# Sorting tokens to their two experts in a graph-attention and mixture-of-experts kernel on Trainium2

## The reference

```python
x = x + gnn(layernorm(x), inlayer2, adj, ...)
#   h = inlayer2 @ W.T + b;  logits = (h @ w1 + b1)[:, None] + (h @ w2 + b2)[None, :]
#   softmax(leaky_relu(logits) + (-1e9 where adj == 0)) @ layernorm(x)
x = x + ffn(layernorm(x), gate_w, gate_b, W1, b1, W2, b2)
#   probs = softmax(xf @ gate_w + gate_b);  top2_vals, top2_idx = top_k(probs, 2)
#   cw: top2_vals at top2_idx, 0 elsewhere
#   for each expert: out += cw[:, e] * (gelu(xf @ W1[e] + b1[e]) @ W2[e] + b2[e])
```

## Time and profile before

| | |
|---|---|
| three runs | 508.79, 512.33, 513.11 us; median 512.33 |
| profiled execution, span from first to last instruction | 509.6 us; the page gives no other time for it |
| median less that span | 2.7 us |
| TensorE busy / VectorE / ScalarE / POOL | 471.5 / 425.4 / 234.3 / 46.7 us |
| mean granted TensorE clock | 0.980 of 2.4 GHz |
| attention's last result copied by ScalarE | from 320.04 us |

### The profile page before, as it was taken

The page is one execution under the profiler, slowest core; times in us unless marked ns, Lnnn a source line. Parts: engine busy times, 40 slices in busy tenths (PEclk is TensorE's granted clock), DMA queues, the critical chain, the costliest instruction groups (busy, mean ns, idle before and its releaser), DMA issues.

```text
span 509.6 us, 5787 instructions
## 1 busy us (share of the span) xinstructions
PE 471.5 (93%) x1712; PEld 221.2 (43%) x1712; DVE 425.4 (83%) x726; ACT 234.3 (46%) x362; POOL 46.7 (9%) x98
## 2 busy tenths in 40 slices
PE   2799999799979999899998999798999999999996
PEld 2773434245335444454444534343434444444442
DVE  0447679798998998989989897579899898988985
ACT  1539810113200200102001124689888888988883
POOL 8903202001010020020000000100000000000000
PEclk9859999999989999999999999999999999999999
DMA  6999999999809639389000000423443346445520
GB/s 193 183 106 105 105 106 202 168 163 90 76 2 97 66 30 105 31 77 88 0 0 0 1 0 21 153 84 82 104 82 113 124 118 122 84 103 112 126 50 22
DMA packets 35042, 44.49 MB, mean 87 GB/s; under 512 B 2592, under 2 KB 24528, under 8 KB 34768
## 3 DMA queue, kind: packets, MB, share of 16 engines
q0 software_dynamic: 17920, 18.88, 37.4%
q1 hardware_dynamic: 16288, 25.37, 19.7%
q10 hardware_dynamic: 816, 0.03, 0.1%
HBM read 92.38 MB, written 2.23 MB: 186 GB/s over the span
## 4 chain that ended last, share of the span: by engine, by line
PE 55%; DVE 23%; issue 7%; DMA 7%; ACT 6%; DVEq 1%; SPq 0%; ACTq 0%
PE bank L1044 20%; DVE c L828 11%; PE bank L1089 4%; PE bank L1091 4%; PE bank L1090 4%; DMA x<-in_x 4%; PE bank L1078 4%; PE bank L1080 4%; PE bank L1079 4%; DMA share<-in_L_gnn_inlayer 2%; DVE maskT L640 2%; PE bank L966 2%; ACT mask L567 2%; DVE xs L714 2%; DVE maskT L891 2%
## 5 line engine op out<-in xcount | busy, mean ns | idle before, releaser
L1044 PE MATMUL bank<-c,Y 128*128 128x512 f32 x512 | 232.9, 603 | 8.9 <-DVE c L828 8.3
L828 DVE SCALAR_TENSOR_TENSOR c<-g_row,r_col,maskT 128x512 f32<-128x512 f32 (+1 forms) x256 | 182.1, 744 | 17.8 <-PE bank L1044 14.0
L1044 PEld LDWEIGHTS bank<-c,Y 128*128 128x128 f32 x512 | 93.1, 191 | 132.7 <-issue 75.5
L885 DVE TENSOR_TENSOR mask<-mask,share 128x1024 f32<-128x1024 f32 x64 | 78.2, 1223 | 21.0 <-ACT mask L567 18.5
L567 ACT ACTIVATE mask<-bank,b1T 128x512 f32<-128x512 f32 x128 | 83.8, 688 | 22.8 <-PE bank L1080 21.2
L891 DVE TENSOR_TENSOR maskT<-mask,maskT 128x1024 f16<-128x1024 f32 x64 | 78.4, 1225 | 0.0
L574 ACT ACTIVATE maskT<-mask 128x1024 f16<-128x1024 f32 x64 | 67.4, 1053 | 3.2 <-DVE mask L885 3.1
L1089 PE MATMUL bank<-maskT,w2h 128*128 128x512 f16 x128 | 49.1, 383 | 5.7 <-DVE maskT L891 5.2
L1090 PE MATMUL bank<-maskT,w2h 128*128 128x512 f16 x128 | 49.0, 383 | 0.0
L1091 PE MATMUL bank<-maskT,w2l 128*128 128x512 f16 x128 | 49.0, 383 | 0.0
L1078 PE MATMUL bank<-share,w1h 128*128 (+1 forms) x128 | 48.5, 379 | 0.0
(11 more groups left out here) (145 smaller groups left out, 355.4 us busy)
## 6 DMA issues: line engine op xcount, KB each, us to landing
share<-shares SPq DMA_DIRECT2D x16, 1024.0 KB, 8.3
mask<-in_adj POOLq DMA_DIRECT2D x24, 512.0 KB, 17.2
mask<-in_adj POOLq DMA_DIRECT2D x32, 128.0 KB, 25.6
share<-in_L_gnn_inlayer SPq DMA_DIRECT2D x2, 1024.0 KB, 10.0
share<-in_x POOLq DMA_DIRECT2D x8, 256.0 KB, 12.2
out<-c SPq DMA_DIRECT2D x8, 256.0 KB, 3.8
share<-in_L_ffn_W SPq DMA_DIRECT2D x1, 1024.0 KB, 21.6
W_sb<-in_L_gnn_W SPq DMA_DIRECT2D x1, 64.0 KB, 2.0
```

Source lines behind the costliest of these rows:

```text
L828: dve.scalar_tensor_tensor(c[:, k % CR].rearrange("p (s i) -> p s i", i=32), g_row[:, bass.ds(s * ST, ST)].rearrange("p (s i) -> p s i", i ...
L885: dve.tensor_tensor(hw[:, e % 2], h[:, e % 2], wb[:, e].unsqueeze(1).to_broadcast([P, FC, ST]), ALU.mult).then_inc(hw_done, 1)
L1044: mm(bank[:, par, :], Y[:, k], c[:, k % CR], start=(k == 0), stop=(k == NK - 1)).then_inc(c_used, 1)
```

## The change

The experts no longer see every token. Each token's row is written twice to memory, to a place sorted by expert, and the experts work on 46 tiles of 256 sorted rows (27 for the tokens of supertiles 0 to 4, the first group, and 19 for the other three, each expert's part padded to whole tiles).

A row (`rows`, 132 words) holds 128 high and 128 low float16 parts, made as before but not transposed, and the row's own number. After routing, TensorE counts ranks with triangular and all-ones products (`rank`), VectorE turns ranks into row places (`slot_i`) and into the expert of each tile (`expert`). Then:

- POOL writes rows by indirect DMA, 128 at a time, to `sorted_x` (`place_row`, line 501): the first group's 20 chunks once for the first choice and, with 4096 added to their numbers, once for the second. It does so after supertile 6 of the attention has given the places, while supertile 7 runs.
- SP loads a tile (`load_tile`), up to 12 ahead. TensorE transposes it (`turn_x`), ScalarE copies it back (`copy_x`), then `ffn1` with 256 columns, gelu, `high` and `low` (both now on VectorE), and `ffn2` turned about: hidden values stand still and the weights pass, so results come out by token. TensorE and ScalarE read the tile's expert into a register, and weights and biases are addressed by it.
- VectorE adds the split halves of the result out of PSUM (`evict`), and POOL writes 256 result rows, two indirect DMAs, to `choice_y` at the row's number (`place_choice`, line 514). There are 12 buffers.
- Each token's two results are loaded back, weighed by the gate and added to the residual (`load_choices`, `combine`), for five supertiles beside tiles 37 to 41 and for three at the end.
- The second group has 24 row writes (12 chunks, two choices). POOL makes them from tile 18 on, four ahead of each of six tiles' result writes.

All loops are unrolled. The routing of the first group runs in supertile 6 (before: 24 chunks in supertile 7); the low half of six supertiles' rows is made by POOL (`low_rows`).

```diff
-    PEELED = 3
-    LAG = 3
+    LAG = 2
+    RW = D + 4
+    TW = 256
+    TP = TW // P
+    XR = 12
+    YR = 12
+    HR = 3
+    HEAD = 5
+    GROUP = ((0, HEAD * TS), (HEAD * TS, NK))
+    TILES = [(2 * (b - a) * P + E * (TW - 1)) // TW for a, b in GROUP]
+        COMBINE = TILES[0] + 9
+        SECOND = 18
+        STD, LOGIT, EXP, RANK = 2, 7, 9, 15
...
         def _(sp):
-            def share_out(g):
...
-            def share_in(st, half):
...
+            def load_tile(t):
+                if t == 0 or t == TILES[0]:
+                    for s_in in sorted_in[t > 0]:
+                        sp.wait_ge(s_in, 16 * (GROUP[t > 0][1] - GROUP[t > 0][0]))
...
+                if t >= XR:
+                    sp.wait_ge(y_out[(t - XR) % YR], 16 * TP * ((t - XR) // YR + 1))
+                sp.dma_start(xt[:, t % XR].rearrange("p s w -> p (s w)"),
+                             sorted_x[TW * t:TW * t + TW].rearrange("(p s) w -> p (s w)", s=TP)).then_inc(xt_in[t % XR], 16)
...
+            for t in range(NT):
+                load_tile(t)
+                if COMBINE <= t < COMBINE + HEAD:
+                    load_choices(t - COMBINE, TILES[0])
...
         def _(pool):
+            def place_row(r, v, n):
+                pool.indirect_dma_start(out=sorted_x, out_offset=bass.IndirectOffsetOnAxis(ap=slot_i[:, v, n:n + 1].bitcast(U32), axis=0),
+                                        in_=rows_2[:, n - GROUP[1][0]] if (r, v) == (1, 1) else rows[:, n],
+                                        in_offset=None).then_inc(sorted_in[r][v], 16)
...
+            def place_choice(t):
+                pool.wait_ge(y_done, t + 1)
+                for i in range(TP):
+                    pool.indirect_dma_start(out=choice_y, out_offset=bass.IndirectOffsetOnAxis(ap=xt_id[:, t % XR, i, D:D + 1].bitcast(U32), axis=0),
+                                            in_=y_sb[:, t % YR, i], in_offset=None).then_inc(y_out[t % YR], 16)
...
+            pool.wait_ge(slot_ready, 1)
+            for n in range(*GROUP[0]):
+                place_row(0, 0, n)
+            second_ids()
+            for n in range(*GROUP[0]):
+                place_row(0, 1, n)
             pool.wait_ge(xs_ready, NS)
             pool.tensor_copy(x2[:, (NS - 1) * TS:NS * TS, :], xs[:]).then_inc(x2_kept, 1)
+            pool.wait_ge(xld_ready, 2)
+            pool.wait_ge(c_used, NS * NK)
+            pool.tensor_copy(rows_2, rows[:, GROUP[1][0]:NK]).then_inc(ids_moved, 1)
...
+            for t in range(NT):
+                if t == SECOND:
+                    pool.wait_ge(slot_ready, 2)
+                if SECOND <= t < SECOND + 6:
+                    for n in range(GROUP[1][0] + 2 * (t - SECOND), GROUP[1][0] + 2 * (t - SECOND) + 2):
+                        place_row(1, 0, n)
+                        place_row(1, 1, n)
+                place_choice(t)
...
         def _(act):
+            for t in range(NT):
...
+                experts.append(act.value_load(expert[0:1, t:t + 1], min_val=0, max_val=E - 1))
...
+                if t + 1 < NT:
+                    copy_x(t + 1)
+                gelu(t)
...
         def _(dve):
+            def high(t):
+                dve.wait_ge(gelu_done, t + 1)
+                need(dve, ffn2_done, t + 1 - HR)
+                dve.tensor_scalar(hh[:, t % HR], h[:, t % 2], C_SCALE, None, ALU.mult).then_inc(hh_done, 1)
...
+            def evict(t):
...
+                need(dve, y_out[t % YR], 16 * TP * (t // YR))
+                dve.tensor_reduce(y_sb[:, t % YR], both, AX_X, ALU.add).then_inc(y_done, 1)
...
+            for t in range(NT):
+                high(t)
+                if t >= LAG:
+                    evict(t - LAG)
+                low(t)
...
+                if COMBINE + 1 <= t < COMBINE + 1 + HEAD:
+                    combine(t - COMBINE - 1, 0)
+                    combine(t - COMBINE - 1, 1)
+            for t in range(NT - LAG, NT):
+                evict(t)
+            for s in range(HEAD, NS):
+                combine(s, 0)
+                if s > HEAD:
+                    combine(s - 1, 1)
+            combine(NS - 1, 1)
...
         def _(pe):
+                if t == TILES[0]:
+                    pe.wait_ge(expert_ready, 2)
+                experts.append(pe.value_load(expert[0:1, t:t + 1], min_val=0, max_val=E - 1))
+                if t == 0:
+                    turn_x(0)
+                if t + 1 < NT:
+                    turn_x(t + 1)
+                ffn1(t)
+                if t >= LAG:
+                    ffn2(t - LAG)
...
+                if t == RANK:
+                    rank(1)
```

More of the change, by code:

```diff
@@ L600, in _, with copy_x @@
-            for st in range(PEELED):
-                experts(st)
-            with act.Fori(PEELED, NS) as st:
-                experts(st)
-            high(NS * E - 1, E - 1)
-            copy_y(NS - 1)
+            for s in range(1, NS):
+                supertile(s)
+            post_a(NS - 1, 1)
+            act.wait_ge(expert_ready, 1)
+            experts = []
+            def copy_x(t):
+                act.wait_ge(turned_x, t + 1)
+                need(act, h_ready, t - 1)
+                act.activation(xtT[:, t % 2].rearrange("p v t -> p (v t)"), bank[:, 0, 0:TW].bitcast(F16),
+                               ACT.Copy).then_inc(xtT_ready, 1)
@@ L814, in _, with supertile @@
             BN = (12, 13, 17, 18)
             TURNS = (15, 20, 24, 28)
-            def supertile(s, par, n, first=False, last=False):
-                router = route_b(*ROUTE[0])
+            routers = [route_b(r) for r in range(2)]
+            def supertile(s, first=False, last=False):
+                par = s % 2
                 for k in range(NK):
@@ L845, in supertile @@
                         post_b(s - 1, BN.index(k))
-                    if not first and k == 25:
+                    if last and k == 23:
                         post_c(s - 1)
@@ L940, in _ @@
-            for st in range(PEELED):
-                experts(st)
-            with dve.Fori(PEELED, NS) as st:
-                experts(st)
-            low(NS * E - 1, E - 1)
-            add_out(NS - 1)
+            for s in range(NS):
+                supertile(s, first=(s == 0), last=(s == NS - 1))
+            post_0(NS - 1)
+            post_a(NS - 1)
+            post_sum(NS - 1)
+            post_b(NS - 1, 0)
+            dve.wait_ge(post_step, (NS - 1) * POST + 1)
+            post_b(NS - 1, 1)
@@ L1052, in supertile @@
                         post_a(s - 1)
[L1053 removed]
+                    if not first and k == 24:
                         post_b(s - 1)
[L1055 removed]
+                    if not first and k == 27:
                         post_c(s - 1)
[L1057 to L1058 removed]
+                    if s == HEAD + 1 and k == 20:
+                        rank(0)
             pe.wait_ge(b1_copied, 1)
@@ L1133 @@
+            for t in range(NT - LAG, NT):
+                ffn2(t)
 _INS = ["x", "adj", "L0_gnn_inlayer2", "L0_gnn_W", "L0_gnn_b", "L0_gnn_w1", "L0_gnn_b1", "L0_gnn_w2", "L0_gnn_b2",
```

692 lines of the change are left out of this document (363 added, 329 removed).

## The result

The changed kernel takes 567.63 us (median of 4 runs, 566.11 to 568.35) against 511.41 us for the kernel before (median of 4 runs) on the same chip. The ratio is 1.110, with a 95% interval of 1.106 to 1.115. The forecast was 497, its range ended at 540.

What follows compares the result with a forecast made beforehand. TensorE was taken to bound the expert part (189.6 us). Attention ends at 319, first products 329.5, tile 27 at 417.9, tiles and combining 475.4, tail 494.7; with 2.7 more, 497 us (3% faster), range 470 to 540.

Steps and rivals of the forecast that it cites:

- p: Price of one indirect write by POOL, taken as 0.85 us, between 0.54 and 1.3.
- 112 writes on the path: POOL's writes standing in line on the path where p exceeds 0.89: 40 + 36 + 34 + 2.
- step 3: Tiles 0 to 17: 45 us plus 10 woven in, second slots at 384.5; POOL's 36 result writes end at 383.1.
- Rival A: POOL is the bound, p 1.0 or more: time 513 at 1.0, 535 at 1.2; chance 0.26.
- Step 1: Attention, with routing moved earlier and POOL making low halves (under 3 us), ends at 319 (311 to 326).
- VectorE's interference: First 40 row writes, beside two-input VectorE mask steps, would each wait some 0.3 us: 12 us more, 509.
- rival B: The tile itself is dear, c 3 or more, by register loads or lower clock: 516 at 3.0, 535 at 3.5; chance 0.20.
- What is woven in: Beside tiles 0 to 17: ScalarE table loads, the last supertile's normalisation and VectorE routing steps, 10 us.
- c: Time of one tile of 256 sorted tokens, taken as 2.5 us, between 1.65 and 4.35.
- The tail: At the end: two writes and landing 4.2, six loads 9, combine 2.3, store 3.8 us, to 494.7.
- The clock: TensorE's products run near half rate after a wait; each of the two stalls costs 1 to 2 us so.
- Steps 2 and 4: First and second groups' row writes: TensorE stalls 9 us before the first tile and 13 us before tile 27.

Runs made afterwards that it cites:

- the run with five forms: Changed kernel plus twenty extra indirect writes of five row counts and sizes into unread memory, other engines standing still; 592.89 us (one run).
- 16 and 16 version: Changed kernel with groups of 16 and 16 token blocks, bias split and row writes moved, VectorE pausing, second-group copy dropped; 519.70 us, ratio 1.018.

## Why the prediction was wrong

**The term that was mis-sized: p.** "I take 0.85: the middle of the direct ones beside VectorE plus POOL's smallest read of a column." It is 1.27 at rest. The bounds (0.54 to 1.3) held that, though not the 1.37 beside VectorE; the value did not. The nearest rows were direct DMAs, whose pitch said nothing on the fixed work of an indirect one; and "nothing in the rows shows reading 128 offsets to be as dear as that" looked for the price in the offsets, while the run with five forms puts all but some 0.1 us into the instruction itself. With the prediction's own count of 112 writes on the path, 112 x (1.275 - 0.85) = 47.6 us, of which 1.4 fall into the slack that its step 3 had (383.1 against 384.5): 497 becomes 543. Rival A, with a chance of 0.26, said so: place, count and break-even at 1.0. Its reason, VectorE beside POOL, is the smaller part: the price is 1.27 with the other engines at rest.

**The wait that was missing.** Step 1 (attention's end at 319) counted POOL's low halves at under 3 us and did not follow POOL's program to what stands ahead of them: the bias split, with a load behind both weight loads on SP's queue. Its removal gave 17.3 us (14.5 at the first row write) and put the attention's end at 317.4, where the step had 319. Against the forecast's first slots the wait made 13 us.

**The held write.** The prediction left VectorE's interference out of its sum and weighed it in rival A, at 0.3 us for each of 40 writes. The trace shows one write held for 6.7 us more and the others by 0.0 to 0.7. The Trainium skill (SBUF — State Buffer, Who interferes with whom) says that VectorE instructions with two SBUF inputs contend with POOL instructions that read SBUF, and that in VectorE's two-port mode whoever came first blocks the other for one whole instruction. The runs agree in so far as the hold goes with VectorE's run, but it lasted over several of VectorE's instructions, so this rule does not explain it.

**The sum, and what is left.** On the clock of the traced execution 494.7 + 46.2 + 13 + 6.7 makes 560.6 of the 564.4. Most of the rest lies behind tile 27: from there to the last tile's two writes 62.4 us passed, and 57.5 were forecast. The prediction let the tiles set the pace there and counted only the last two of POOL's 44 writes in that stretch. In the trace POOL pauses no longer than 0.31 us from 493.1 to its last write at 548.0: its writes set the pace there too.

**Right, in part by luck.** Step 3: 55 us from the first products to the second slots were forecast, 56 measured (365.6 to 421.6), but the two terms behind it are off in opposite ways. An undisturbed tile takes 1.85 us, not 2.5 (the columns alone were put at 1.65), so rival B (3 or more) is out, and 18 tiles make 33 us, not 45. What is woven in, with the lower clock after the first stall, took the other 23, not 10:

```profile
365.00:391.00 26.00, 19.55 (x152) 14.86 (x153) 13.88 (x35) 17.70 (x33) 4.46 (x5) 0.78 0.23 62
```

The 600 ns register load that the prediction cited from the Trainium skill (DMA: Bandwidth & Descriptors, Latency and other measured facts) would have made c 2.95; no run here shows that load by itself, and the undisturbed tile is well below. POOL's first result was forecast 23 us after the first products and came 22.9 us after the first transposes, by luck again: the 4.7 us copy took 1.50, and a wait of 12.4 us for VectorE's low half ahead of it filled the time. The tail, 19.3 from the last tile's two writes to the end, came to 17.7 (546.7 to 564.4). The clock: after the second stall, at 0.50 and then 0.89, the first tiles started 3.41 and 2.21 us apart instead of 1.85: 1.9 us lost, within the 1 to 2 forecast.

**Steps 2 and 4,** the stalls of 9 and 13 us, became 34 and 49, by p and the held write: the order of events in them is as forecast, and POOL's 36 result writes, "just in time" at 0.85, were 16 us late at 1.37. Some 6 us of the second stall are no loss: TensorE was through 27 tiles in 69 us where 75 were forecast.

## What to carry to other kernels

Before work is moved to an engine in an instruction that the trace has never shown, count its instances on the path and compute the value at which the change loses; where that lies inside the bounds (here 1.0 in 0.54 to 1.3), the forecast is a guess about one number, and the way to know it is one run of that instruction alone. A saving on the bound engine (here 113 us of TensorE's columns by the prediction's count) is worth only what the new chain lets through: from slots over row writes to the first load of the next group. And follow the program of an engine that gets a new duty from its top: what waits ahead of the duty becomes part of it.

## What the runs showed of the hardware

- An indirect write from POOL, with the other engines at rest, cost 0.97 to 0.99 us and a pause of 0.30 for 128 rows of 128, 512 or 2112 bytes; 0.90 for 64 rows, 0.87 for 32. The rows landed some 2.3 us after the issue.
- A write that began in VectorE's gapless run behind the slots took 7.69, 7.47, 4.76 or 4.75 us (8.27 in the 16 and 16 version) and ended 0.15 to 0.97 us after VectorE's first pause had begun; why is open. Most writes beside VectorE are not held: 19 of the first 20 in the changed kernel took 0.97 to 1.62.
- Six POOL operations on 2 partitions x 1024 took 1.03 to 2.85 us each, five of them over 2.1; a subtraction took 2.11 there and 1.14 on 128 partitions x 512. Few partitions did not make them cheap.
- A tile of half the size took the same 1.85 to 1.9 us.
